# A mixture-of-experts first layer on TensorE: two 64-row half products for a pair of blocks, in place of the fifth whole product of each block

## The reference, cut to what matters

```
cap = 2 * 1.25 * N / E        # N = 4096 tokens, E = 8 experts: 1280 rows for each expert
xb  = einsum('nec,nd->ecd', sec_mask, xf)               # rows sent to each expert, [8, 1280, 192]
h   = gelu(einsum('ecd,edf->ecf', xb, fc_w) + fc_b)     # first layer, 192 -> 768
out = einsum('ecf,efd->ecd', h, pj_w) + pj_b            # second layer, 768 -> 192
y   = einsum('nec,ecd->nd', cb_weight, out)
```

## Time and profile before

| | us |
|---|---|
| median of 3 runs | 1197.01 (1195.33 to 1200.75) |
| the profiled execution, its own time | 1199.42 |
| its span, first to last instruction | 1197.6 |
| TensorE busy with matmuls | 989.5 (83%) |
| VectorE, ScalarE, GpSimd busy | 671.0, 707.3, 465.3 |
| stretch of the experts, from its first expert product to its last instruction | 856.2 to 1197.6 |

### The profile page before, as it was taken

How to read it: one execution, slowest core, us unless ns; L and a number is a source line. 1 busy time by engine, 2 the same in 40 slices (tenths; PEclk the granted TensorE clock), 3 DMA queues, 4 the chain that set the end, 5 groups by cost and what they waited for, 6 DMA issues and landing times.

```text
span 1197.6 us, 22280 instructions
## 1 busy us (share of the span) xinstructions
PE 989.5 (83%) x7325; PEld 742.8 (62%) x7326; DVE 671.0 (56%) x3071; ACT 707.3 (59%) x1547; POOL 465.3 (39%) x508
## 2 busy tenths in 40 slices
PE   1256889988997888998888889765499999999996
PEld 1144566555665556665665665435398988888886
DVE  2344878888876666656655746538244333334331
ACT  2024888888887867766776868626234433543432
POOL 5666645444010000222222202120365576667554
PEclk7586999999998969899998999955699999999999
DMA  8222122111000000011011011113655354564442
GB/s 203 40 40 44 31 37 31 25 28 25 2 1 1 2 1 2 1 32 32 2 32 31 2 32 33 32 31 55 110 76 102 71 111 76 94 89 85 70 51 30
DMA packets 58116, 53.60 MB, mean 45 GB/s; under 512 B 14462, under 2 KB 52256, under 8 KB 58016
## 3 DMA queue, kind: packets, MB, share of 16 engines
q0 software_dynamic: 26112, 27.89, 17.0%
q1 hardware_dynamic: 31904, 24.47, 7.6%
HBM read 35.94 MB, written 16.39 MB: 44 GB/s over the span
## 4 chain that ended last, share of the span: by engine, by line
PE 64%; ACT 11%; DVE 8%; issue 8%; POOL 6%; DMA 3%; POOLq 0%; ACTq 0%; DVEq 0%
PE ps_ring L682 12%; PE ps_scores L682 11%; PE ps_ring L674 11%; PE ps_ring L906 9%; PE ps_scores L780 5%; PE ps_ctx L797 5%; POOL got L505 4%; PE ps_scores L906 4%; PE ps_scores L783 2%; ACT probs L1022 2%; PE ps_ring L737 2%; PE ps_ring L736 1%; ACT ctx_t L1037 1%; ACT probs L1030 1%; DMA got<-place_rows,id_now 1%
## 5 line engine op out<-in xcount | busy, mean ns | idle before, releaser
L1119 ACT ACTIVATE probs<-ps_scores,fc_bias 128x512 f32<-128x512 f32 (+1 forms) x144 | 88.5, 618 | 160.6 <-PE ps_scores L682 151.9
L556 POOL DMA_INDIRECT out<-z_t,slots_now x80 | 129.9, 1624 | 113.7 <-DVE z_t L1556 90.4
L674 PE MATMUL ps_ring<-ident,probs 128*128 128x128 f32 x768 | 128.1, 292 | 19.7 <-DVE x_hi L1186 9.4
L1004 ACT ACTIVATE prob_t<-ps_ring 128x512 f32<-128x512 f32 x192 | 114.9, 599 | 40.0 <-PE ps_ring L674 38.6
L682 PE MATMUL ps_ring<-x_hi,w_hi 128*128 128x512 f32 x240 | 110.0, 458 | 33.4 <-DVE k L1192 11.2
L1269 DVE CUSTOM_DVE_ANT_0 probs<-ps_scores,causal 128x128 f32<-128x128 f32 x384 | 89.0, 287 | 74.6 <-PE ps_scores L783 73.4
L906 PE MATMUL ps_ring<-work,probs 128*128 128x192 f32 x672 | 117.1, 328 | 7.0 <-issue 3.8
L674 PEld LDWEIGHTS ps_ring<-ident,probs 128*128 128x128 f32 x768 | 93.6, 149 | 45.7 <-issue 14.6
L1013 ACT ACTIVATE square<-ps_scores 128x512 f32<-128x512 f32 x192 | 104.7, 601 | 28.3 <-DVE row_max L1263 13.0
L1030 ACT ACTIVATE probs<-probs,neg_max 128x128 f32<-128x128 f32 x384 | 120.8, 395 | 0.6 <-DVE neg_max L1269 0.6
L906 PEld LDWEIGHTS ps_ring<-work,probs 128*128 128x128 f32 x672 | 109.4, 190 | 10.4 <-issue 10.4
(11 more groups left out here) (208 smaller groups left out, 2257.7 us busy)
## 6 DMA issues: line engine op xcount, KB each, us to landing
work<-pj_w SPq DMA_DIRECT2D x8, 576.0 KB
token_in<-xin SPq DMA_DIRECT2D x8, 384.0 KB, 3.5
out<-resid SPq DMA_DIRECT2D x8, 384.0 KB, 4.3
vals<-fc_w SPq DMA_DIRECT2D x8, 384.0 KB
vals<-fc_w SPq DMA_DIRECT2D x16, 192.0 KB
out<-z_t,slots_now POOLq DMA_INDIRECT x80
token_in<-xin SPq DMA_DIRECT2D x8, 128.0 KB, 4.2
got<-pj_b SPq DMA_DIRECT2D x8, 96.0 KB, 7.1
```

Source lines behind the costliest of these rows:

```text
L556: gp.indirect_dma_start(out[:, :], bass.IndirectOffsetOnAxis(slots_now[:, u, 1, t:t + 1], 0), slot_y[:, o, :], None, compute_op=ALU.add).t ...
L674: return pe.transpose(dst, src, ident[0:n, 0:n])
L1004: sc.activation(prob_t[:, s % 2, :, :], src.rearrange("p (h q) -> p h q", h=4), ACT.Exp if p is mag else ACT.Copy).then_inc(ring_free[i], 1)
L1119: sc.activation(hidden[:, c % 2, f_, 0:128 * nt], ps_scores[:, i, 0:128 * nt], ACT.Gelu, bias=fc_bias[:, e, f_:f_ + 1]).then_inc(gelu_done ...
```

## The change

A block gets four whole products instead of five. The fifth term is done for two blocks at once by two 64-row products, one on partitions 0 to 63 for the first block, one on partitions 64 to 127 for the second. For this, part 1 is laid out anew. `x_hi[:, 1]` holds x hi in both halves, a new `x_low[:, 1]` holds x lo in both, and `fc_lo[:, u, 1]` holds w hi in its lower half and w lo in its upper. So the fourth whole product gives x hi·w hi and x hi·w lo, and the half product gives x lo·w hi. The term x lo·w lo of part 1 is no longer formed. TensorE now waits for two gelus ahead of each pair of blocks. VectorE's two differences of `split_x` become one over 512 elements, and the subtraction of `split_weights` becomes a copy of 64 x 768, a subtraction of 64 x 768 and one of 128 x 768.

```
-        x_lo = sb("x_lo", [128, GROUP * 128], F32R)
+        x_low = sb("x_low", [128, 2, GROUP * 128], F32R)
+        x_lo = x_low[:, 0, :]
...
-                for f_ in range(FF_CHUNKS):
-                    i = f_ % FC_RING
-                    pe.wait_ge(gelu_done[i], e * 6 + 2 * c + f_ // FC_RING + 1)
-                    col = slice(128 * f_, 128 * f_ + 128)
-                    split_product(ps_scores[:, i, tok], (x_hi[:, 0, tok], x_lo[:, tok], x_hi[:, 1, tok]),
-                                  (fc_hi[:, u, 0, col], fc_lo[:, u, 0, col], fc_hi[:, u, 1, col],
-                                   fc_lo[:, u, 1, col]), False,
-                                  begun=pj_used[1 - u] if c == 0 and f_ == 0 else None).then_inc(fc_full[i], 1)
+                for f_ in range(0, FF_CHUNKS, 2):
+                    for k in range(2):
+                        i = (f_ + k) % FC_RING
+                        pe.wait_ge(gelu_done[i], e * 6 + 2 * c + (f_ + k) // FC_RING + 1)
+                    for k in range(2):
+                        half_rows = slice(REST * k, REST * k + REST)
+                        last = pe.matmul(ps_scores[:, (f_ + k) % FC_RING, tok],
+                                         fc_hi[half_rows, u, 1, 128 * (f_ + k):128 * (f_ + k) + 128],
+                                         x_low[half_rows, 1, tok], start=True, stop=False, skip_group_check=True)
+                    if c == 0 and f_ == 0:
+                        last.then_inc(pj_used[1 - u], 1)
+                    for k in range(2):
+                        i, col = (f_ + k) % FC_RING, slice(128 * (f_ + k), 128 * (f_ + k) + 128)
+                        pairs = ((fc_hi[:, u, 0, col], x_hi[:, 0, tok]), (fc_lo[:, u, 0, col], x_hi[:, 0, tok]),
+                                 (fc_hi[:, u, 0, col], x_low[:, 0, tok]), (fc_lo[:, u, 1, col], x_hi[:, 1, tok]))
+                        for n, (w, x) in enumerate(pairs):
+                            last = pe.matmul(ps_scores[:, i, tok], w, x, start=False, stop=(n == 3),
+                                             skip_group_check=True)
+                        last.then_inc(fc_full[i], 1)
...
-                    ve.tensor_tensor(fc_lo[:, u, :, :], raw_fc, f(fc_hi[:, u, :, :]), ALU.subtract
+                    hl = slice(REST, 128)
+                    ve.tensor_copy(fc_lo[0:REST, u, 1, :], f(fc_hi[0:REST, u, 1, :]))
+                    ve.tensor_tensor(fc_lo[hl, u, 1, :], raw_fc[hl, 1, :], f(fc_hi[hl, u, 1, :]), ALU.subtract)
+                    ve.tensor_tensor(fc_lo[:, u, 0, :], raw_fc[:, 0, :], f(fc_hi[:, u, 0, :]), ALU.subtract
                                      ).then_inc(raw_split, 1)
...
-                        ve.tensor_tensor(x_lo[:, tok], x_full[:, 0, :], f(x_hi[:, 0, tok]), ALU.subtract)
-                        ve.tensor_tensor(x_hi[hl, 1, tok], x_full[hl, 1, :], f(x_hi[hl, 1, tok]),
-                                         ALU.subtract).then_inc(ex_turn_free[m % 2], 1)
+                        ve.tensor_tensor(x_low[:, :, tok], x_full[:, :, :], f(x_hi[:, :, tok]), ALU.subtract
+                                         ).then_inc(ex_turn_free[m % 2], 1)
```

More of the change, by code:

```diff
@@ L1531, in split_x @@
                     take_weights(e, u, c)
-                    hl = slice(REST, 128)
                     for m in range(t0 // 2, (t0 + nt) // 2):
```

## The result

The changed kernel takes 1224.44 us (median of 4 runs, 1219.06 to 1229.21) against 1197.35 (4 runs of the kernel before): a ratio of 1.0222, with a 95% interval of 1.0161 to 1.0283. Timed once more beside the experiments it took 1219.65 against 1195.80, ratio 1.0154, interval 1.0056 to 1.0252. The forecast was 1216, slower, range 1206 to 1226.

A forecast was written before the change was run, and what follows sets the result against it. TensorE was taken to bound the experts' stage. Terms 14.9 - 1.6 - 2.7 + 1.0 + 4.0 + 3.3 = +18.9 us, against the median of 1197.0, gave 1216 us; range for 8 times in 10: 1206 to 1226.

The forecast's parts named there:

- The islands' price: Each pair's two 64-row products among whole ones (an island) cost 0.40 us beside one product's time: +14.9 us in sum.
- Side by side: Two half products on different rows and into different banks run together, priced as one product plus 0.01 us.
- halves in turn: Rival: the two half products run one after the other, +13.3 us, 1229 us in all; chance 0.06.
- First pairs: At each expert's start TensorE was idle, so the way in and one load were already paid: -1.6 us.
- VectorE's split: Split of x: two differences become one, saving 0.34 us at each of 8 expert starts: -2.7 us.
- The split of weights, hidden: VectorE's new weight split takes up to 1.1 us more, but idle time behind it covers this: no cost.
- The gelu waits: TensorE's waits ahead of second and third pairs: +1.0 at 512 columns, +4.0 at 256, +3.3 behind three table loads.
- the long release: Upper bound for the gelu waits: TensorE needs 0.25 us after a gelu's end instead of 0.05, 9.6 us more.
- hidden loads: Rival: weight loads lie under earlier matmuls, an island costs 0.19 us, +4.8, 1202 us; chance 0.06.
- the free island: Rival: switching to half products costs nothing, but gelu waits grow to 12.6 us; -3.9, 1193 us; chance 0.04.

The follow-up runs named there:

- experiment 2: Changed kernel with the two half products moved between the first block's four whole products and the second's: 1212.15 us against 1198.24 for the kernel before, ratio 1.0123.
- experiment 1: Five whole products per block in the old order with the old waits, only VectorE's changes kept: 1193.59 us against 1198.24 for the kernel before, ratio 0.9949.
- experiment 3: Changed kernel with both half products on partitions 0 to 63: 1232.21 us against 1198.24 for the kernel before, ratio 1.0300.
- experiment 8: Changed kernel with the two gelu waits of a pair in the other order: 1228.38 us, one run.

## Why the prediction was right, and where it was short

The direction, the mechanism and the range of 1206 to 1226 held; the size came out too small, +18.9 us against 23.0 in the stage. The forecast's own narrower range, 1209 to 1223, missed the median of 1224.4, though not the second timing of 1219.65. How near either comes is in part luck: 8 us more or less lie in attention. Step by step:

- **The islands' price, +14.9.** Right. The four parts were forecast as 0.09, 0.10, 0.09 and 0.11; the steps measured (0.33 in by experiment 2, 0.43 out, 0.34 to the next) agree within 0.01 each. Experiment 2 less experiment 1 gives 16.0 (13.9 in the last seven experts, of which the forecast had 13.0). What carried it is that the earlier trace rows showed each part at another place of the same trace.
- **Side by side.** Right: 0.49 us for both; experiment 3 adds 12.5 us to the stage where 13.3 was forecast for halves in turn.
- **First pairs, -1.6.** Right. From an expert's first start to the one after two further products it took 0.56 us before and 0.77 after, in the mean of experts 1 to 7: the island costs 0.21 there instead of 0.40. It fits experiment 2, whose first pairs do not have this: the waits of 12.2, less 0.45 that experiment 2 keeps at two table loads, less 1.6 give 10.2, where the two stages differ by 10.0.
- **VectorE's split, -2.7.** Right in experiment 1 (0.37 at a start). In the changed kernel the mean gain at seven starts is only 0.25 us, some 1.8 in all. Into experts 1 to 5 the halves start 0.24 after VectorE's end and not 0.14; into experts 1 and 4 a rounding on VectorE also took 0.67 and 0.63 us instead of 0.43, in both traces. Neither was foreseen, and the cause of neither is known.
- **The split of weights, hidden.** Right: it is in no wait of TensorE.
- **The gelu waits, +8.3.** This is the term that was mis-sized: it measured 11.8, namely 3.6 at 512 columns (forecast 1.0), 5.1 at 256 (4.0) and 3.1 at the table loads (3.3). At 256 columns in the second pair the step was 0.47 where 0.21 + 0.25 was forecast, right. But in 30 of the 48 waits, the third pairs of the loop and both of experts 6 and 7, TensorE goes on 0.14 after the gelu's end, not 0.05; that is 2.7 of the missing 3.5. I had given the long release of the earlier trace rows as the upper bound, with 9.6 more, and took the short one everywhere. In chunk 0 of experts 0 to 5 the gelu also starts 0.60 after the block's last product instead of 0.53, and once, in expert 7, 0.81; why is open. Two table loads were as forecast, a step of 1.68 instead of 0.35; the first falls into the low clock, where products stand 0.43 apart, and the step was 1.13.

The terms as measured, 14.9 - 1.6 - 1.8 + 11.8, give 23.3 where the stage grew by 23.0.

The rivals: halves in turn (1229) falls by experiment 3, hidden loads (1202) and the free island (1193) by the steps of 0.43 and 0.34. That the median of 1224.4 is nearer to 1229 than to 1216 says nothing for the first of them: it lies between two runs of 1219 to 1220 and two of 1229, and in the profiled one, 1228.9, the experts began 6.6 us late. The profiles of the changed kernel with the first expert product at 862.7 and 854.5 differ by 8.3 us ahead of the stage and by 0.3 in it.

A half and a whole product share rows, so of the rule that the Trainium skill states in "TensorE: Matmul & The Clock Gate", Part 3, The mechanism, only the clause on the background weight buffer could have hidden the loads at a change. The trace does not agree with it there: in experiment 2 the halves' load starts at 1002.09 with their matmul at 1002.10, and the whole product behind them takes 0.50 us instead of 0.39. Between whole products the loads are hidden, as that clause has it. The same page's Part 3, in "Measured speedup vs the span model", puts about 4 ns between packed matmuls. The trace agrees: the two halves start 3 to 4 ns apart.

## What to carry to other kernels

Price a switch between whole and row-tiled products from the steps between starts on both sides: here 0.40 us a visit, so halving one product of 0.23 us could not pay. Count again who waits for whom when instructions are put in groups: moving two waits to the front of a pair cost 10 to 12 us of the 23, and putting the island between the blocks gave 10 back. And look whether the new layout of the data is worth having without the new instructions: five whole products with the single difference are 0.5% faster than the kernel before, of which the traces of the experts show about 2.6 us.

## What the hardware showed that I had not expected

- The order of two waits ahead of a matmul changes the lag behind the later one: 0.14 against 0.05 us, about 3 us in the stage (experiment 8, one run).
- Executions of the kernel before differ by up to 18 us (1193.6 to 1211.4 in 19 runs), and where profiles differ it is in stretches of attention at a lower granted clock, and at the start of the experts' first chunk, which moved the stage by 1.2 us between two traces of the same code (341.4 and 340.2). The last seven experts repeat within 0.3 us (297.3 and 297.3, 317.7 and 317.4). A stage cut out of two profiles behind that point told the change to a few tenths of a microsecond; the medians alone would have needed many runs.
